# Two-layer graph network on one Trainium2 core: gate steps of the third pass one place earlier, and the mixing block's temporaries in the accumulator

## The chip, the cores and the metric

The kernel runs on one core of one Trainium2 chip. A time is that of one execution on the device, in microseconds (us), lower is better. A core has five engines with instruction streams of their own: TensorE (PE, matmuls; its weight loads are listed as PEld), VectorE (DVE), ScalarE (ACT), GpSimd (POOL) and SyncE (SP). [...] An engine takes its instructions strictly in the order in which they stand, so one that waits holds up all behind it.

## The reference

Two layers of a graph network over 6250 nodes with 256 features and 106250 edges, sorted by destination. Each layer adds to x a graph part, a mixing part and a feed-forward part. The change lies in the second layer:

```python
xn = _layernorm(x, axis=-1)
x = x + _L1_gnn_ref(xn, L1_gnn_W_self, L1_gnn_W_neigh, L1_gnn_b, src, dst) + _L1_mix_ref(xn[None], L1_mix_w_qkv, ...)[0]
x = x + _L1_ffn_ref(_layernorm(x, axis=-1)[None], L1_ffn_sW1, ...)[0]

# in _L1_mix_ref, over all nodes at once
attn = jax.nn.softmax(jnp.einsum('bhnd,bhne->bhde', k, v), axis=-1)
x = x + xf                                 # xf = attn applied to q
h = _layernorm(x, norm_g, norm_b)
h = jax.nn.gelu(h @ w_fc1 + b_fc1, approximate=False) @ w_fc2 + b_fc2

# in _L1_ffn_ref: one shared MLP and 4 experts, of which 2 count
gates = jax.nn.softmax(x @ gW + gb, axis=-1)
topv, topi = jax.lax.top_k(gates, TOPK)
topw = jax.nn.softmax(topv, axis=-1)
gated = jnp.sum(sel * topw[:, :, None, :], axis=-1)
return shared + gated
```

The graph part is a mean over each node's incoming edges of the rows of xn @ W_neigh, plus xn @ W_self + b.

## The kernel before

The nodes are 49 tiles of 128 rows (`T`), kept in the tile `XN`. The edges are 880 groups of 128, called visits (`VIS`). The kernel is a row of blocks. A block begins when all engines have ended the one before.

Three blocks are passes over the 880 visits, the third for the second layer. For each visit GpSimd fetches 128 source rows of 256 floats from a table in memory into one of 16 slots of the tile `rows` (line 1847), TensorE multiplies them with a 128x128 matrix of zeros and ones (line 1940), and VectorE adds the product to its place in `ACC`, the first 12544 columns of the large tile `AR` (line 2056). The profile shows each fp32 matmul as two. The results of two visits share a PSUM bank, two banks alternate, and VectorE adds a pair when its second visit is done. TensorE may begin a pair when the pair before the last one has been added (`s_av`, `x - 2`).

Beside the visits each pass does the dense work of the tiles. `turns` (line 732) sets the order, the same on every engine: turn `i` has places q = 0 to 17 and one place `QN` at the end; at each place first `side(i, q)` is issued, then one visit (18 or 19 to a turn, 18.3 on average). In turn `i` the third pass serves tile `i + 1` (`na`) for the mixing block's front and its norm, tile `i` (`b`) for its MLP, tile `i - 1` (`s`) for the norm ahead of the feed-forward part, and tile `i - 2` (`f`) for that part. An even or odd start of the turn's visits decides at which places the pairs end.

The chain of one tile `f` runs over all engines:

- TensorE q = 3: the gate's logits (L1978) into bank 7, and the first layer's product group 0 (`first_ffn`, L1955); q = 4: groups 1, 2; q = 5: group 3, then a wait until VectorE has read the logits (`lg`), since group 4 writes the same part of bank 7; then group 4; q = 6: group 5.
- VectorE q = 4: gate steps 0 and 1 (L2100, L2102; the second signals `lg`); q = 6: steps 2, 3; q = 7: steps 4, 5; q = 8, 9: steps 6 to 9; q = 10: `weights` (ends with L2135 and the signal `wg`). ScalarE takes the two exponentials at q = 5 and q = 8.
- TensorE q = 12: transposes the gate weights (L2013, waits for `wg`). VectorE q = 13: copies them out of PSUM (L2174, signals `wtc`). TensorE q = 14: spreads them (L2023, waits for `wtc`). VectorE q = 15: applies them (L2178).

Of another kind is the short block before the third pass (from line 1702): a serial chain of small matmuls and copies that makes the mixing block's 256x512 matrix from sums over all nodes. Its weights and temporaries lie in `rows`. GpSimd clears `ACC` there (line 1719). TensorE begins when all eight loads of the block have landed and GpSimd's three fills are done (lines 1731, 1732). The gathers of the third pass begin in the next block, since they write `rows`.

## Time and profile before

| | |
|---|---|
| median of 3 runs | 4081.71 us (4075.95 to 4083.36) |
| profiled execution | 4071.0 us |
| its span | 4069.3 us |
| mean granted TensorE clock | 0.895 |
| PE busy | 3277.6 us (81%) |
| DVE busy | 2367.5 us (58%) |
| ACT busy | 1846.6 us (45%) |
| POOL busy | 2698.7 us (66%) |

All rows come from the one profiled execution. Times are from the start of its span. Busy shares over the whole span are averages over stages with different limits. In this execution the short block begins at 2767.3 us and the third pass at about 2811 us, and the last instruction ends a few microseconds before 4069.3 us.

### The profile page before, as it was taken

The numbers are of one execution on the slowest core, as the hardware profiler recorded it, in microseconds if no ns is written. First come the engines' busy times: TensorE is split into PE (matmuls) and PEld (weight loads), VectorE is DVE, ScalarE is ACT, GpSimd is POOL, SyncE is SP. The second block draws the span as 40 slices with busy tenths as digits, with TensorE's granted clock in tenths as the row PEclk, the third lists the DMA queues.
The fourth block names the chain that finished last, engine by engine and source line by source line (L and its number), as shares of the span: only waits on it lengthen the run. The fifth ranks groups of instructions, "written<-read, shape, count | busy, mean of one in ns | idle before, by whom it ended". The sixth has DMA issues, their size and how long they took to land. (4 is left out here: it accounts for less than half of the span.)

```text
span 4069.3 us, 58095 instructions
## 1 busy us (share of the span) xinstructions
PE 3277.6 (81%) x15028; PEld 2486.5 (61%) x15028; DVE 2367.5 (58%) x8479; ACT 1846.6 (45%) x4614; POOL 2698.7 (66%) x2858
## 2 busy tenths in 40 slices
PE   7767666766666787888888888776999999999998
PEld 4544444444444465666667666664777777777777
DVE  6444444444444455666666665363777777777776
ACT  4344444444443444544445442132555555555554
POOL 4177777777776777777777773043776676666762
PEclk9677877787877788999999998886999999999999
DMA  4353333333333434666666666642333333333331
GB/s 123 95 159 111 112 110 111 110 112 110 110 112 97 118 120 141 192 194 203 200 193 197 194 193 223 201 136 75 109 104 101 101 102 102 101 101 101 103 101 48
DMA packets 268651, 532.12 MB, mean 131 GB/s; under 512 B 57942, under 2 KB 165653, under 8 KB 268199
## 3 DMA queue, kind: packets, MB, share of 16 engines
q0 software_dynamic: 139296, 386.65, 32.2%
q1 hardware_dynamic: 129030, 141.78, 11.0%
q8 instruction: 126, 2.06, 0.2%
q14 instruction: 199, 1.62, 0.1%
HBM read 463.88 MB, written 64.34 MB: 130 GB/s over the span
## 5 line engine op out<-in xcount | busy, mean ns | idle before, releaser
L1847 POOL DMA_INDIRECT rows<-table,src_idx x880 | 845.0, 960 | 388.2 <-issue 219.9
L786 POOL DMA_INDIRECT rows<-table,src_idx x880 | 835.3, 949 | 268.1 <-issue 265.4
L1061 POOL DMA_INDIRECT rows<-table,src_idx x880 | 835.2, 949 | 267.9 <-issue 253.5
L880 DVE TENSOR_TENSOR AR<-AR,ps 128x256 f32 x880 | 370.6, 421 | 592.3 <-PE ps L837 529.1
L1224 DVE TENSOR_TENSOR AR<-AR,ps 128x256 f32 x880 | 370.1, 421 | 329.1 <-PE ps L1135 244.4
L1940 PE MATMUL ps<-rows,AR 128*128 128x256 f32 x1760 | 538.6, 392 | 7.9 <-issue 3.6
L2056 DVE TENSOR_TENSOR AR<-AR,ps 128x256 f32 x880 | 369.2, 420 | 177.2 <-PE ps L1940 101.6
L837 PE MATMUL ps<-rows,work 128*128 128x256 f32 x880 | 315.0, 486 | 172.9 <-DMA rows<-table,src_idx 151.7
L1135 PE MATMUL ps<-rows,work 128*128 128x256 f32 x1168 | 362.6, 419 | 74.4 <-DMA rows<-table,src_idx 64.9
L837 PEld LDWEIGHTS ps<-rows,work 128*128 128x128 f32 x880 | 188.0, 238 | 272.2 <-issue 141.9
L1940 PEld LDWEIGHTS ps<-rows,AR 128*128 128x128 f32 x1760 | 285.8, 193 | 72.0 <-issue 50.3
L1135 PEld LDWEIGHTS ps<-rows,work 128*128 128x128 f32 x1168 | 221.5, 208 | 151.6 <-issue 105.0
L797 ACT ACTIVATE work<-iota,dst_rel 128x128 f32<-128x128 f32 x440 | 140.5, 390 | 231.7 <-PE ps L837 231.4
L837 PE MATMUL ps<-rows,mring 128*128 128x256 f32 x440 | 163.8, 501 | 100.5 <-DMA rows<-table,src_idx 92.5
L1135 PE MATMUL ps<-rows,mring 128*128 128x256 f32 x592 | 186.7, 420 | 72.0 <-DMA rows<-table,src_idx 66.0
L1176 PE MATMUL ps<-wreg,work 128*128 128x512 f32 x392 | 209.3, 662 | 30.1 <-DVE work L1328 15.2
L1111 ACT ACTIVATE AR<-AR 128x1024 f32<-128x1024 f32 x49 | 51.8, 1057 | 393.9 <-DVE AR L1341 393.9
L837 PE MATMUL ps<-rows,gates 128*128 128x256 f32 x440 | 163.6, 500 | 83.1 <-DMA rows<-table,src_idx 67.7
L1092 ACT ACTIVATE work<-iota,dst_rel 128x128 f32<-128x128 f32 x584 | 185.8, 391 | 84.1 <-PE ps L1135 84.1
L1955 PE MATMUL ps<-AR 128*128 128x128 f32 x1176 | 176.0, 282 | 22.5 <-DVEq L2104 21.6
L837 PEld LDWEIGHTS ps<-rows,mring 128*128 128x128 f32 x440 | 97.3, 245 | 153.7 <-issue 79.6
L1955 PEld LDWEIGHTS ps<-AR 128*128 128x128 f32 x1176 | 159.9, 191 | 37.2 <-DVEq L2104 29.0
(508 smaller groups left out, 6687.0 us busy)
## 6 DMA issues: line engine op xcount, KB each, us to landing
AR<-in_L_ffn_Wd SPq DMA_DIRECT2D x48, 1024.0 KB, 7.2
rows<-table,src_idx POOLq DMA_INDIRECT x2640, 2.8
AR<-h_sorted SPq DMA_DIRECT2D x52, 512.0 KB, 3.9
table<-AR SPq DMA_DIRECT2D x147, 128.0 KB, 2.2
AR<-in_x SPq DMA_DIRECT2D x4, 1536.0 KB
out_x<-XN SPq DMA_DIRECT2D x48, 128.0 KB
AR<-in_L_ffn_bd SPq DMA_DIRECT2D x40, 128.0 KB, 8.3
y_sorted<-AR SPq DMA_DIRECT2D x40, 128.0 KB
```

The costliest lines, as they stand in the source:

```text
L786: g.indirect_dma_start(out=rows[:, u * D:(u + 1) * D], out_offset=None, in_=table[0], in_offset=bass.IndirectOffsetOnAxis(ap=src_idx[:, x: ...
L837: ins = pe.matmul(pair(x), hot[Q % 4][:, x % 4 * P:(x % 4 + 1) * P], rows[:, x % RING * D:(x % RING + 1) * D], start=True, stop=True)
L880: v.tensor_tensor(acc, acc, pair(y), ALU.add).then_inc(s_av, 1)
L1061: g.indirect_dma_start(out=rows[:, u * D:(u + 1) * D], out_offset=None, in_=table[1], in_offset=bass.IndirectOffsetOnAxis(ap=src_idx[:, x: ...
L1092: ins = a.activation(hot[Q % 3][:, k * P:(k + 1) * P], iota[:, :], ACT.Abs, scale=-1.0, bias=dst_rel[:, 4 * Q + k:4 * Q + k + 1])
L1135: ins = pe.matmul(pair(x), hot[Q % 3][:, x % 4 * P:(x % 4 + 1) * P], rows[:, x % RING * D:(x % RING + 1) * D], start=True, stop=True)
L1176: ins = pe.matmul(ps[3 + h][:, :], f_xT[:, c * P:(c + 1) * P], ff1[:, c, h * 512:(h + 1) * 512], start=c == 0, stop=c == 1)
L1224: v.tensor_tensor(acc, acc, pair(y), ALU.add).then_inc(s_av, 1)
L1847: g.indirect_dma_start(out=rows[:, u * D:(u + 1) * D], out_offset=None, in_=table[2], in_offset=bass.IndirectOffsetOnAxis(ap=src_idx[:, x: ...
L1940: ins = pe.matmul(ps[x // 2 % 2][:, x % 2 * D:(x % 2 + 1) * D], hot[Q % 4][:, x % 4 * P:(x % 4 + 1) * P], rows[:, u * D:(u + 1) * D], star ...
L1955: ins = pe.matmul(f_l1(k), w, f_xT[:, c * P:(c + 1) * P], start=c == 0, stop=c == 1)
L2056: v.tensor_tensor(acc, acc, ps[x // 2 % 2][:, y % 2 * D:(y % 2 + 1) * D], ALU.add).then_inc(s_av, 1)
```

## The change

Five edits, all in the second layer's last two blocks.

1. TensorE: product group 4 and the wait for `lg` go from q = 5 to q = 6; the transpose of the gate weights goes from q = 12 to q = 11.
2. VectorE: gate steps 4, 5 go from q = 7 to q = 6, steps 6 to 9 from q = 8, 9 to q = 7, 8, `weights` from q = 10 to q = 9, and the copy of the gate weights from q = 13 to q = 12.
3. ScalarE: the second exponential goes from q = 8 to q = 7.
4. Short block: its large temporaries lie in the first 3856 columns of `ACC`, and the first 16 gathers of the third pass are issued there. GpSimd's order is: two small fills, 16 gathers, then zeros over the columns of `ACC` from 3856 on. TensorE waits for three of the eight loads (`s_wq`) and two fills.
5. Third pass: VectorE clears the first 3856 columns of `ACC` as its first instruction and waits for that.

```diff
+        s_gr = [sem(f"j_g{u}") for u in range(RING // 2)]
+        ATMP = 3856
+
+        def gather3(g, x):
+            u = x % RING
+            g.indirect_dma_start(out=rows[:, u * D:(u + 1) * D], out_offset=None, in_=table[2],
+                                 in_offset=bass.IndirectOffsetOnAxis(ap=src_idx[:, x:x + 1], axis=0)).then_inc(s_gr[u // 2], 16)
-        wqkv = rows[:, 0:1536].rearrange("p (c n) -> p c n", c=2)
+        wqkv = ACC[:, 0:1536].rearrange("p (c n) -> p c n", c=2)
...
             @block.gpsimd
             def _(g):
-                g.memset(ACC, 0.0).then_inc(s_z3, 1)
-                g.memset(rows[:, 3072:3328], 0.0).then_inc(s_z3, 1)
+                g.memset(ACC[:, 3072:3328], 0.0).then_inc(s_z3, 1)
                 g.memset(nval, float(N)).then_inc(s_z3, 1)
+                for x in range(RING):
+                    gather3(g, x)
+                g.memset(ACC[:, ATMP:T * D], 0.0).then_inc(s_z3, 1)
...
             @block.tensor
             def _(pe):
-                pe.wait_ge(s_w, 8 * 16)
-                pe.wait_ge(s_z3, 3)
+                pe.wait_ge(s_wq, 3 * 16)
+                pe.wait_ge(s_z3, 2)
...
@@ third pass, ScalarE @@
-                    if q == 8 and has(f):
                         a.wait_ge(*pr.after(f))
                         a.wait_ge(*wg.room(f))
                         a.activation(x4, p4, ACT.Exp, bias=n2).then_inc(e2.sem, 1)
@@ third pass, TensorE @@
                     if q == 5 and has(f):
                         first_ffn(f, (3,)).then_inc(l1a.sem, 1)
+                    if q == 6 and has(f):
                         pe.wait_ge(*lg.after(f))
-                        first_ffn(f, (4,))
-                    if q == 6 and has(f):
-                        first_ffn(f, (5,)).then_inc(l1.sem, 1)
+                        first_ffn(f, (4, 5)).then_inc(l1.sem, 1)
...
-                    if q == 12 and has(f):
                         pe.wait_ge(*wg.after(f))
                         pe.transpose(ps[7][0:NG + 1, D:D + P], f_w, ident[:, :]).then_inc(wt.sem, 1)
@@ third pass, VectorE @@
+                v.memset(ACC[:, 0:ATMP], 0.0).then_inc(s_az, 1)
+                v.wait_ge(s_az, 1)
...
                     if q == 6 and has(f):
-                        gate(f, 2)
-                        gate(f, 3)
-                    if q == 7 and has(f):
-                        gate(f, 4)
-                        gate(f, 5)
-                    if q in (8, 9) and has(f):
-                        gate(f, 2 * q - 10)
-                        gate(f, 2 * q - 9)
-                    if q == 10 and has(f):
+                        for k in range(2, 6):
+                            gate(f, k)
+                    if q in (7, 8) and has(f):
+                        gate(f, 2 * q - 8)
+                        gate(f, 2 * q - 7)
+                    if q == 9 and has(f):
                         weights(f)
...
-                    if q == 13 and has(f):
+                    if q == 12 and has(f):
                         v.wait_ge(*wt.after(f))
                         v.wait_ge(*l3.room(f))
                         v.tensor_copy(f_wT, ps[7][0:NG + 1, D:D + P]).then_inc(wtc.sem, 1)
```

In the listings of order below, a line number is that of its own program, so the same instruction has another one in the changed kernel. TensorE, places 3 to 7 of a turn in the middle of the pass, before (L1940 a visit, L1978 logits, L1955 the groups, two matmuls each, L1993 the mixing matrix):

```order
L1978 MATMUL ps<-AR 128x4 x2
L1955 MATMUL ps<-AR 128x128 x2
L1940 MATMUL ps<-rows,AR 128x256
L1955 MATMUL ps<-AR 128x128 x4
L1940 MATMUL ps<-rows,AR 128x256
L1955 MATMUL ps<-AR 128x128 x4
L1940 MATMUL ps<-rows,AR 128x256
L1955 MATMUL ps<-AR 128x128 x2
L1940 MATMUL ps<-rows,AR 128x256
L1993 MATMUL ps<-AR 128x512 x2
```

The same places now (L1949 a visit, L1987 logits, L1964 groups, L2001 mixing matrix):

```order
L1987 MATMUL ps<-AR 128x4 x2
L1964 MATMUL ps<-AR 128x128 x2
L1949 MATMUL ps<-rows,AR 128x256
L1964 MATMUL ps<-AR 128x128 x4
L1949 MATMUL ps<-rows,AR 128x256
L1964 MATMUL ps<-AR 128x128 x2
L1949 MATMUL ps<-rows,AR 128x256
L1964 MATMUL ps<-AR 128x128 x4
L1949 MATMUL ps<-rows,AR 128x256
L2001 MATMUL ps<-AR 128x512 x2
```

The wait for `lg` stood inside the third L1955 row, ahead of its second group; now it stands behind the third visit, ahead of the fourth L1964 row. TensorE, places 11 to 14, before (L2006, L2008 the second layer, L2013 the transpose of the gate weights, L2017 the mixing MLP's second product, L2023 the spreading):

```order
L2006 MATMUL ps<-AR 128x128 x2
L2008 MATMUL ps<-AR 128x128 x4
L1940 MATMUL ps<-rows,AR 128x256
L2013 MATMUL ps<-ident,AR 5x128
L1940 MATMUL ps<-rows,AR 128x256
L2017 MATMUL ps<-wreg,AR 128x256 x2
L1940 MATMUL ps<-rows,AR 128x256
L2017 MATMUL ps<-wreg,AR 128x256 x2
L2023 MATMUL ps<-AR 128x128 x2
```

And now (L2014, L2016, L2020, L2024, L2030 in that order):

```order
L2014 MATMUL ps<-AR 128x128 x2
L2016 MATMUL ps<-AR 128x128 x4
L2020 MATMUL ps<-ident,AR 5x128
L1949 MATMUL ps<-rows,AR 128x256 x2
L2024 MATMUL ps<-wreg,AR 128x256 x2
L1949 MATMUL ps<-rows,AR 128x256
L2024 MATMUL ps<-wreg,AR 128x256 x2
L2030 MATMUL ps<-AR 128x128 x2
```

The transpose has passed one visit; the spreading stands where it stood. VectorE, places 12 and 13 of a turn whose pairs end at odd places, before (L980, L975, L977 steps of two norms, L2174 the copy of the gate weights, L2056 the adding of a visit):

```order
L980 SCALAR_TENSOR_TENSOR gsml<-gsml 128x1
L975 TENSOR_SCALAR gsml<-gsml 128x1
L977 SCALAR_TENSOR_TENSOR gsml<-gsml 128x1 x2
L980 SCALAR_TENSOR_TENSOR gsml<-gsml 128x1
L977 SCALAR_TENSOR_TENSOR gsml<-gsml 128x1
L2174 COPY AR<-ps 5x128
L2056 ISA
L2056 TENSOR_TENSOR AR<-AR,ps 128x256
```

And now (L2180 the copy, L2065 the adding):

```order
L980 SCALAR_TENSOR_TENSOR gsml<-gsml 128x1
L975 TENSOR_SCALAR gsml<-gsml 128x1
L977 SCALAR_TENSOR_TENSOR gsml<-gsml 128x1
L2180 COPY AR<-ps 5x128
L977 SCALAR_TENSOR_TENSOR gsml<-gsml 128x1
L980 SCALAR_TENSOR_TENSOR gsml<-gsml 128x1
L977 SCALAR_TENSOR_TENSOR gsml<-gsml 128x1
L2065 ISA
L2065 TENSOR_TENSOR AR<-AR,ps 128x256
```

The copy has passed three norm steps. In a turn whose pairs end at even places it passes the two adds of a pair as well.

## Rows read from the trace of the kernel before

**Rows 1.** A stretch: from:to, us, busy us of each engine, granted clock, DMA.
```profile
3300.00:3500.00 200.00, 187.86 (x1071) 153.93 (x1069) 147.74 (x579) 107.20 (x280) 140.41 (x146) 1.00 0.35 101
```
**Rows 2.** Waits, 2900 to 4069 us: waiter, releaser, us in total, times, longest.
```profile
POOL rows L1847 <- PE ps L1940: 133.7, 153, 2.9
DVE AR L2056 <- PE ps L1940: 93.2, 132, 2.5
PE ps L2023 <- DVE AR L2174: 36.3, 44, 1.5
PE ps L1955 <- DVEq L2104: 21.6, 35, 1.2
PE ps L2013 <- DVEq L2137: 5.6, 12, 0.5
```
**Rows 3.** PE in order of time: start, us, what [idle before, releaser].
```profile
3576.29 0.60 PE L1940 MATMUL ps<-rows,AR 128*128 128x256 f32 x2
...
3580.50 0.71 PE L1955 MATMUL ps<-AR 128*128 128x128 f32 x4 [0.52 <-DVEq L2104]
3581.05 0.60 PE L1940 MATMUL ps<-rows,AR 128*128 128x256 f32 x2
3581.48 0.61 PE L1955 MATMUL ps<-AR 128*128 128x128 f32 x4
...
3594.40 0.71 PE L2023 MATMUL ps<-AR 5*128 5x128 f32 x4 [1.18 <-DVE AR L2174]
...
3971.70 0.71 PE L2023 MATMUL ps<-AR 5*128 5x128 f32 x4 [1.32 <-DVE AR L2174]
```
**Rows 4.** DVE in order of time, the same turn.
```profile
3575.10 0.96 DVE L2056 TENSOR_TENSOR AR<-AR,ps 128x256 f32 x2
...
3581.78 0.97 DVE L2056 TENSOR_TENSOR AR<-AR,ps 128x256 f32 x2 [1.02 <-PE ps L1940]
...
3593.49 0.35 DVE L977 SCALAR_TENSOR_TENSOR gsml<-gsml 128x1 f32<-128x1 f32 x2
...
3594.08 0.27 DVE L2174 COPY AR<-ps 5x128 f32<-5x128 f32 x1
```
**Rows 5.** DVE, a turn whose pairs end at even places.
```profile
3389.88 0.97 DVE L2056 TENSOR_TENSOR AR<-AR,ps 128x256 f32 x2
...
3391.23 0.27 DVE L2174 COPY AR<-ps 5x128 f32<-5x128 f32 x1
```
**Rows 6.** Short block in order of time, all engines.
```profile
2767.32 10.55 POOL L1719 MEMSET AR<- 128x12544 f32 x1 [33.15 <-POOLq L1538]
...
2778.21 0.18 PEld L1734 LDWEIGHTS ps<-ident,rows 128*128 128x128 f32 x1 [14.06 <-DMA wreg<-in_L_mix_b_fc]
2778.24 0.45 PE L1734 MATMUL ps<-ident,rows 128*128 128x128 f32 x1 [13.69 <-POOL rows L1721]
...
2789.35 0.69 DVE L1778 COPY rows<-ps 128x512 f32<-128x512 f32 x1 [9.27 <-PE ps L1745]
...
2809.30 0.69 DVE L1809 TENSOR_TENSOR AR<-AR 128x512 f32<-128x512 f32 x1
```
**Rows 7.** DMA from 2765 to 2812 us, 40 slices of 1.175 us.
```profile
GB/s 144 79 32 230 392 236 369 327 365 79 0 0 0 0 0 0 0 0 0 0 0 0 0 0 0 0 0 0 0 0 0 0 0 0 0 0 0 0 0 0
```
**Rows 8.** Start of the third pass in order of time, all engines.
```profile
2812.44 0.94 POOL L1847 DMA_INDIRECT rows<-table,src_idx  x1 [0.30 <-issue]
2813.69 0.94 POOL L1847 DMA_INDIRECT rows<-table,src_idx  x1 [0.30 <-issue]
...
2818.17 0.69 DVE L2160 TENSOR_TENSOR AR<-ps,AR 128x512 f32<-128x512 f32 x1 [6.02 <-PE ps L1993]
...
2861.09 0.67 PE L1940 MATMUL ps<-rows,AR 128*128 128x256 f32 x2 [1.27 <-DMA rows<-table,src_idx]
```
**Rows 9.** Two stretches at low clock, columns as in rows 1.
```profile
2884.70:2888.10 3.40, 3.40 (x9) 2.25 (x8) 2.81 (x9) 0.00 (x0) 2.79 (x3) 0.51 0.39 112
3973.50:3980.30 6.80, 6.80 (x16) 4.58 (x15) 3.43 (x12) 0.00 (x0) 3.26 (x4) 0.50 0.16 45
```

More of the change, by code:

```diff
@@ L1680, in _ @@
                         v.sem_inc(s_nf, 1)
-        wqkv = rows[:, 0:1536].rearrange("p (c n) -> p c n", c=2)
-        gram = rows[:, 1536:2048].rearrange("p (c n) -> p c n", c=2)
-        t1 = rows[:, 2048:2560].rearrange("p (c n) -> p c n", c=2)
-        wq1T = rows[:, 2560:3072].rearrange("p (c n) -> p c n", c=2)
-        abd = rows[:, 3072:3328].rearrange("p (c n) -> p c n", c=2)
-        abT = rows[:, 3328:3584].rearrange("p (c n) -> p c n", c=2)
-        bqc = rows[:, 3584:3586]
-        bqm = rows[:, 3600:3728]
-        csum, nmx = rows[:, 3586:3588], rows[:, 3588:3590]
-        rsm = rows[:, 3590:3592]
-        nval = rows[0:1, 3592:3593]
-        att = rows[:, 3728:3856].rearrange("p (c n) -> p c n", c=2)
+        s_gr = [sem(f"j_g{u}") for u in range(RING // 2)]
[5 more added lines that the diff above has]
+        wqkv = ACC[:, 0:1536].rearrange("p (c n) -> p c n", c=2)
+        gram = ACC[:, 1536:2048].rearrange("p (c n) -> p c n", c=2)
+        t1 = ACC[:, 2048:2560].rearrange("p (c n) -> p c n", c=2)
+        wq1T = ACC[:, 2560:3072].rearrange("p (c n) -> p c n", c=2)
+        abd = ACC[:, 3072:3328].rearrange("p (c n) -> p c n", c=2)
+        abT = ACC[:, 3328:3584].rearrange("p (c n) -> p c n", c=2)
+        bqc = ACC[:, 3584:3586]
+        bqm = ACC[:, 3600:3728]
+        csum, nmx = ACC[:, 3586:3588], ACC[:, 3588:3590]
+        rsm = ACC[:, 3590:3592]
+        nval = ACC[0:1, 3592:3593]
+        att = ACC[:, 3728:3856].rearrange("p (c n) -> p c n", c=2)
         bqkv = work[0:1, 0:768]
@@ L1777, in _ @@
                 v.wait_ge(s_p, 5)
-                link(v.tensor_copy(rows[:, 2048:2560], ps[1][:, :]))
+                link(v.tensor_copy(ACC[:, 2048:2560], ps[1][:, :]))
                 link(v.tensor_copy(t2row, ps[2][0:1, 0:D]))
@@ L1786, in _ @@
                 v.wait_ge(s_p, 8)
-                link(v.tensor_copy(rows[:, 2560:3072], ps[4][:, :]))
+                link(v.tensor_copy(ACC[:, 2560:3072], ps[4][:, :]))
                 v.wait_ge(s_a, 2)
@@ L1797, in _ @@
                 v.wait_ge(s_p, 10)
-                link(v.tensor_copy(rows[:, 3328:3584], ps[5][:, 0:D]))
+                link(v.tensor_copy(ACC[:, 3328:3584], ps[5][:, 0:D]))
                 v.wait_ge(s_p, 14)
@@ L1809, in _ @@
                 link(v.tensor_tensor(gws[:, :, D:2 * D], gws[:, :, D:2 * D], gws[:, :, 0:D], ALU.add))
-        s_gr = [sem(f"j_g{u}") for u in range(RING // 2)]
+        s_az = sem("j_acc_zero")
         s_mv, s_av, s_abs, s_hota, s_hotv = (sem("j_" + n) for n in "visit added abs hot_a hot_v".split())
@@ L1842, in _ @@
             def _(g):
-                for x in range(VIS):
-                    u = x % RING
-                    if x >= RING and x % 2 == 0:
+                for x in range(RING, VIS):
+                    if x % 2 == 0:
                         g.wait_ge(s_mv, (x + 2 - RING) // 2)
-                    g.indirect_dma_start(out=rows[:, u * D:(u + 1) * D], out_offset=None, in_=table[2],
-                                         in_offset=bass.IndirectOffsetOnAxis(ap=src_idx[:, x:x + 1], axis=0)).then_inc(s_gr[u // 2], 16)
+                    gather3(g, x)
             @block.scalar
```

14 lines of the change are left out of this document (8 added, 6 removed).

## The prediction

> **What bounds the kernel now.** I read first the busy times by stretch, to see which engine is near its limit in the stage that the change touches; then the waits of that stage, summed; then one turn in order of time on TensorE and on VectorE; last the short block and its DMA traffic.
>
> [...] GpSimd issues a gather every 1.25 us if it waits for nothing [rows 8]: 22.9 us a turn. It isn't the bound, and it waits for TensorE 133.7 us in all [rows 2]. TensorE's own waits are the three last lines of rows 2: 36.3 us for the copy of the gate weights, 21.6 us for gate step 1 (`lg`), 5.6 us for `weights`. [...] So TensorE bounds the pass, held up by VectorE at two places of each turn where VectorE happens to be late, while at other places VectorE waits for it. [...]
>
> **The wait for the copy (L2174).** In the turn shown TensorE stands 1.18 us before L2023, and goes on 0.32 us after the copy starts [rows 3, 4]. The copy now stands ahead of three norm steps: 3593.62 instead of 3594.08 (the second of the two L977 that start at 3593.49), so 0.46 us sooner. In a turn whose pairs end at even places it also passes the two adds: 3389.88 instead of 3391.23, 1.35 us sooner [rows 5]. Half the turns are of each kind. The same view for all 46 turns with visits gives waits of 0.88 us on average in the 24 turns of the second kind, of which about 20.5 us in all go, and 0.74 us in the 22 of the first kind, of which 0.45 us go each, 10 us. Together 30 of some 38 us. The copy can't be held up by its own input: the transpose ahead of it moves one place too.
>
> **The wait for `lg`.** It moves behind one visit, 0.43 us of TensorE work (3581.05 to 3581.48) [rows 3]. 35 waits make 21.6 us [rows 2]; each loses 0.43 us or all it has: 14 us go, some 7 stay. Group 4 isn't needed sooner, since `l1` was signalled behind group 5 before as well. Behind the wait that is now at q = 6 stand groups 4, 5 and the next visit, as many as before less one.
>
> **The wait for `weights`** (L2013). On VectorE `weights` passes the place q = 9 with its norm steps and often a pair's adds (0.97 us, rows 4), on TensorE the transpose passes one visit (0.43 us). So it gains more than it loses: 5 of the 5.6 us go. The moved gate steps cost no new time. Until q = 9 VectorE does about 0.8 us more of its work than before, and has it less afterwards. Before the adds at q = 5 it stands idle for 1.02 us in the turn shown [rows 4], and the visit there now runs ahead of TensorE's wait instead of behind it, so those adds can begin sooner. If that idle time were not there, the 0.8 us would push the adds back; they would still be ahead of the visit that needs them, two pairs later. ScalarE takes its exponential one place sooner, at 54% busy: nothing.
>
> First order: 30 + 14 + 5 = 49 us.
>
> **What is late next.** The end of a turn on VectorE. In the turn shown the last pair's adds end at 3575.10 + 0.96 = 3576.06, and the third visit of the next turn, which needs them, starts at 3576.29 [rows 3, 4]: 0.23 us of room. TensorE comes some 0.85 us sooner at q = 14 and VectorE not by all of it. I take that 0.5 us come back as a new wait in each of the 22 turns of this kind, 11 us. Less than nothing can't come back. At the other end VectorE keeps its idle places and all that the copy's move brings TensorE from q = 14 on comes back, 0.8 us in each of 46 turns, 37 us. So the pass gives 38 us, bounds 12 and 50.
>
> **The short block.** TensorE starts at 2778.24, when GpSimd's fill of 10.55 us and the two small ones are done; the loads are also just down, its weight load names one of them [rows 6]. Now it needs two small fills and three loads, 0.79 MB. By its slices, from the first load at about 2767.7 [rows 7], 0.27, 0.46 and 0.28 MB move until 2769.7, 2770.9 and 2772.05, so these three are down at about 2771.1 and, with the 1.3 us that lie between the end of traffic (2776.9) and the start at 2778.2, seen at 2772.4: 5.8 us sooner. The gathers are beside them now, 128 KB every 1.25 us or 105 GB/s against some 300: about 1.3 us later. I take 4.5 us; the bounds are 0 (the loads no sooner than all eight were) and 5.8. The chain behind, to the end of L1809 at 2809.99 [rows 6], is the same instructions on other columns. GpSimd needs 0.4 us of fills, 16 x 1.25 = 20 us of gathers and 10.55 x 8688/12544 = 7.3 us of zeros, so it ends near 2795, 10 us ahead of the chain. VectorE's zeros over 3856 columns are not in the trace; by the copies of 512 columns in 0.69 us [rows 6] some 4 to 5 us, between bounds of 2 and 8 us. They lie at the start of the pass, where VectorE stands idle 6.02 us before L2160 [rows 8], so I take 0; at 8 us they would cost 2.
>
> [...] If gathers and weights shared evenly for the whole load, the three loads would take up to twice their 3.4 us and the block's gain would be 2 instead of 4.5 us. No row of the kernel before has both in flight there.
>
> **The first turns.** With 16 rows fetched early the wait of 1.27 us for a gather at 2861.09 [rows 8] goes: 1.3 us.
>
> **The clock.** [...] TensorE is busy through both stretches, so they cost up to half of 10.2 us. I take 2 us, bounds 0 and 5. [...]
>
> **Sum.** 38 + 4.5 + 1.3 + 2 = 46 us off the profiled execution's 4071.0, so 4025 for such an execution. Its own time is 10.7 us under the median of the three runs, which spread over 7.4 us; the forecast goes by the median: 4081.7 - 46 = 4036 us. About 0.2%, 8 us, is what a measurement of this kernel can tell from no change.
>
> **Rivals.**
> 1. *VectorE becomes the bound.* [...] Against it: its idle places at q = 5 and q = 7 are filled by the change itself. Then the pass gives 12 to 25 us and the rest 2 to 6: a gain of about 22, 4060 us. Chance 0.18.
> 2. *The waits come back elsewhere.* TensorE gets to L2023 sooner and stands as long for the next thing that VectorE, as late as before, delivers: the spread weights' use or the norm's rows. Only the short block and the first turns stay, a gain of 6: 4076 us. For it: VectorE's chain from q = 8 to q = 13 runs with hardly a pause. Against it: the copy itself passes work in every turn, by the listing of order. Chance 0.07.
> 3. *Slower: the turn's end on VectorE.* Its place is the adds of a turn's last pair and the third visit. If the denser gate work leaves VectorE later there by more than the 0.23 us of room plus the 1.07 us a turn (49/46) that the moves give, TensorE stands longer than before. At 0.4 us beyond that point the 46 turns cost 18 us, less 6 of the block: 4094 us. For it: the narrow room. Against it: no instruction is added to a turn. Chance 0.05.
>
> The forecast has 0.70, with its own range 4020 to 4052. The range reaches from 4016 (50 + 5.8 + 1.3 + 5 off, and 4 us for the spread of the medians) to 4068, which takes in most of rival 1. Faster by over 0.2%: 0.70 + 0.18 and 0.01 of rival 2, 0.89. Within 0.2%: 0.07. Slower: 0.04.
>
> **What would show it.** In the new waits the line of the spreading matmuls (L2030) has under 12 us, the one of the product groups on gate step 1 under 10, the transpose near 0. TensorE's first matmul of the short block comes 5 to 8 us after GpSimd's first fill instead of 10.9, and 16 gathers stand in that block. A turn in the middle takes 24.3 us, 1.32 us a visit, with TensorE busy 96 to 97%. A new group of waits of a visit's matmul on the adds shows the part given back, about 11 us. The prediction is wrong if these waits are above 25 us, if the waits for the copy stay, if the short block is no shorter, or if the pass loses its full clock.

## The result, and the profile after

| | before | changed |
|---|---|---|
| median | 4078.83 us (4069.96 to 4083.36, 4 runs) | 4006.7 us (4004.6 to 4010.86, 4 runs) |
| ratio, 95% interval | | 0.9827 (0.9807 to 0.9847) |
| profiled execution | 4071.0 us | 4010.9 us |
| span, mean granted clock | 4069.3 us, 0.895 | 4009.1 us, 0.895 |
| GpSimd's first fill in the short block to the end | 1302.0 us | 1239.2 us |

The kernel is faster by 72 us of the medians in this comparison, where 46 were forecast; the time lies below the forecast's own range (4020 to 4052 us) and below the wider one (from 4016 us). A second comparison (below) gave 66 us. The last row of the table is the steadiest measure: up to the first fill of the short block all kernels here are the same, and that fill came anywhere between 2753.2 and 2769.9 us in eleven profiled executions, while the stretch behind it repeats within 0.5 us (before 1302.0 and 1301.5, changed 1239.2 and 1239.1). By it the change is worth 62.4 to 62.8 us, at the lower end of the first comparison's interval (62 to 79 us) and inside the second's (56 to 70 us).

The middle of the third pass, the stretch of [rows 1]:

```profile
3300.00:3500.00 200.00, 196.02 (x1134) 162.26 (x1135) 153.88 (x607) 114.04 (x299) 147.31 (x154) 1.00 0.38 107
```

TensorE is busy 98%, was 94%, and there are 154 gathers instead of 146: 1.30 us a visit, was 1.37. The mean of 46 turns went from 25.32 to 24.05 us (24.3 forecast). The waits from 2900 us on, as in [rows 2]; first the groups of waits, then the group of the visits' matmuls, whose last figures are the idle time ahead of it, of before (L1940) and after (L1949):

```profile
POOL rows L1688 <- PE ps L1949: 68.7, 115, 1.2
DVE AR L2065 <- PE ps L1949: 21.9, 55, 1.1
PE ps L1964 <- DVEq L2113: 5.2, 16, 0.7
PE ps L2030 <- DVE AR L2180: 3.3, 8, 0.5
```
```profile
L1940 PE MATMUL ps<-rows,AR 128*128 128x256 f32 x1636 | 499.1, 389 | 1.5 <-issue 1.3
```
```profile
L1949 PE MATMUL ps<-rows,AR 128*128 128x256 f32 x1628 | 491.2, 388 | 8.0 <-issue 7.1 <-DVE AR L2065 0.2
```

The copy's wait fell from 36.3 to 3.3 us, that for gate step 1 from 21.6 to 5.2, the transpose's is gone. 6.5 us came back ahead of the visits. VectorE waits for the visits' matmuls 21.9 us instead of 93.2. It is still TensorE that bounds the pass, so rivals 1 and 3 of the prediction did not come.

The short block, all engines, against [rows 6]; the last row answers to the memset that had no row before:

```profile
2769.91 0.31 POOL L1728 MEMSET AR<- 128x256 f32 x1 [33.14 <-POOLq L1538]
...
2775.51 0.47 PE L1745 MATMUL ps<-ident,AR 128*128 128x128 f32 x1 [8.35 <-DMA AR<-in_L_mix_b_qkv]
...
2790.38 7.36 POOL L1732 MEMSET AR<- 128x8688 f32 x1
...
2795.66 2.11 DVE L1796 TENSOR_SCALAR AR<-AR 128x2 f32<-128x2 f32 x1
...
2808.53 0.69 DVE L1821 TENSOR_TENSOR AR<-AR 128x512 f32<-128x512 f32 x1
...
2811.53 3.27 DVE L2046 MEMSET AR<- 128x3856 f32 x1 [2.31 <-issue]
```

TensorE starts 5.6 us after the first fill, was 10.9. But L1796, an operation on 2 columns, takes 2.11 us, and it ends 0.03 us after GpSimd's fill (2797.74). So the chain ends 39.3 us after the first fill instead of 42.7: 3.4 us sooner, not 5.3.

### The profile page after: what moved, and what is told of

Read it like the earlier page. It is cut to its first block and busy times, and to the rows that moved or that the text cites. A ratio compares the mean times of both kernels' runs of the same rounds, so it can differ in the third digit from the quotient of the medians.

```text
span 4009.1 us, 58097 instructions
## 1 busy us (share of the span) xinstructions
PE 3268.3 (82%) x15028; PEld 2483.5 (62%) x15028; DVE 2371.8 (59%) x8480; ACT 1843.5 (46%) x4614; POOL 2701.9 (67%) x2858
## 5 line engine op out<-in xcount | busy, mean ns | idle before, releaser
L1949 PE MATMUL ps<-rows,AR 128*128 128x256 f32 x1760 | 532.4, 391 | 12.6 <-issue 10.4
L2065 DVE TENSOR_TENSOR AR<-AR,ps 128x256 f32 x880 | 368.8, 419 | 110.3 <-PE ps L1949 25.9
L1949 PEld LDWEIGHTS ps<-rows,AR 128*128 128x128 f32 x1760 | 287.2, 192 | 82.9 <-issue 58.3
L837 PE MATMUL ps<-rows,mring 128*128 128x256 f32 x440 | 160.6, 493 | 93.2 <-DMA rows<-table,src_idx 82.1
L1158 PE MATMUL ps<-AR 128*128 128x256 f32 x640 | 172.3, 397 | 9.8 <-DMA AR<-in_L_ffn_bd 9.8
L837 PEld LDWEIGHTS ps<-rows,gates 128*128 128x128 f32 x440 | 96.3, 241 | 131.7 <-issue 71.0
```

Source lines behind the costliest of these rows:

```text
L837: ins = pe.matmul(pair(x), hot[Q % 4][:, x % 4 * P:(x % 4 + 1) * P], rows[:, x % RING * D:(x % RING + 1) * D], start=True, stop=True)
L1158: ins = pe.matmul(ps[6][:, 0:D], XHT[:, k * P:(k + 1) * P], XW[b % 2][:, k * D:(k + 1) * D], start=k == 0, stop=k == HC - 1)
L1949: ins = pe.matmul(ps[x // 2 % 2][:, x % 2 * D:(x % 2 + 1) * D], hot[Q % 4][:, x % 4 * P:(x % 4 + 1) * P], rows[:, u * D:(u + 1) * D], star ...
L2065: v.tensor_tensor(acc, acc, ps[x // 2 % 2][:, y % 2 * D:(y % 2 + 1) * D], ALU.add).then_inc(s_av, 1)
```

## The experiments

All ratios are to the kernel before, measured in the same session. The sessions fell under two conditions: under the first the kernel before takes 4072 to 4074 us as in the result, under the second 4677 to 4686. The record gives a chip number with every session of experiments, and number 1 stands with both conditions, so it is not shown that the two are two chips.

For most of the runs under the first condition I took TensorE's matmuls in order of time from the q = 0 transposes of tile 2 to those of tile 48, 46 turns, called turns 2 to 48 below by that tile. Each gap of over 0.02 us is put down to the line behind it (us; "low clock" is the time at a granted clock of 0.50 within these turns; "rest" is the length less the idle time and half the low clock):

| kernel | copy | gate step 1 | transpose | visits, first 7.5 us of a turn | visits, later | all idle | low clock | rest | length | first fill to end |
|---|---|---|---|---|---|---|---|---|---|---|
| before | 36.9 | 21.6 | 6.0 | 6.2 | 1.4 | 77.1 | 13.7 | 1080.7 | 1164.7 | 1302.0 |
| before_again | 36.8 | 21.8 | 6.0 | 6.2 | 1.0 | 77.3 | 6.8 | 1081.8 | 1162.5 | 1301.5 |
| lg_again | 37.1 | 7.1 | 6.1 | 6.4 | 1.4 | 63.2 | 23.9 | 1078.4 | 1153.5 | 1290.4 |
| dvecopy12 | 1.8 | 22.5 | 17.4 | 6.8 | 0.9 | 54.5 | 0 | 1079.4 | 1133.9 | 1272.2 |
| copy_again | 3.7 | 22.9 | 0 | 6.6 | 6.4 | 44.5 | 3.4 | 1079.5 | 1125.7 | 1262.5 |
| moves_again | 3.4 | 7.1 | 0 | 6.6 | 5.4 | 27.4 | 3.4 | 1078.0 | 1107.2 | 1243.6 |
| after_again | 3.3 | 6.3 | 0 | 6.2 | 5.8 | 26.9 | 3.4 | 1077.6 | 1106.2 | 1239.1 |
| weights_behind | 0.3 | 6.3 | 0 | 7.5 | 1.7 | 21.0 | 0 | 1074.3 | 1095.2 | 1229.6 |

**after_again and before_again.** The two kernels unchanged.

> The changed kernel once more, on a chip where its parts were or can be timed. Theory A (the parts add: the moves' waits, the short block and nothing else): its gain over the kernel before is that of the moves plus that of the block, so 21 + 16 = 37 to 45 us on a chip like the one of the single edits (ratio 0.990 to 0.992), and 60 to 72 us on one like that of the first result. Theory B (part of the gain comes only when all edits stand together, because TensorE then waits nowhere long enough for the clock to dip): more than the sum by 10 us or more. In the profile both expect under 30 us of idle time of TensorE in turns 2 to 48 on a chip like the first, against 77 before; theory B also expects no stretch at 0.5 in the third pass, where the kernel before has one or more.

> The kernel before once more, for its profile on this chip beside those of the other kernels. Nothing changed: ratio 1.000 within 0.3%. If the dips of the granted clock in the third pass are chance, they lie elsewhere or are not there; if they follow the waits for the copy, there are one or more again, each behind a wait of over 1.2 us on L2023.

4007.09 us, ratio 0.9845 (0.9828 to 0.9862), 63 us; the kernel before gave 0.9996 (0.9984 to 1.0008). The gain is 62.4 us by profile; moves_again beside it has 57.9. So 4.5 us are left for the short block and for whatever comes only when all edits stand together, and theory B's 10 us are ruled out. The waits of before repeat to 0.2 us.

**moves_again.** Edits 1 to 3 alone, the third pass's order:

```diff
-                    if q == 13 and has(f):
+                    if q == 12 and has(f):
                         v.wait_ge(*wt.after(f))
...
```

> Gate steps, copy of the gate weights and product group moved; temporaries, zeros and gathers as in the kernel before. By the prediction's working the moves bring 38 to 40 us. By the account of the two first traces (turns 2 to 48 shorter by 58 us, of which 50 are idle time of TensorE that is gone and 8 a shorter busy time) they bring 58 us, a ratio of 0.9858, on a chip like that of the first result; the rest of the change is then worth 4 to 6 us. On a chip where the before kernel takes 4677 us they brought 21 to 26 us.

4015.58 us, ratio 0.9862 (0.9845 to 0.9879), 56 us. The moves bring 56 to 58 us, the short block and the early gathers the other 4.5 by profile. The short block's edits were not run alone under the first condition.

**lg_again.** One wait and one product group:

```diff
                     if q == 5 and has(f):
                         first_ffn(f, (3,)).then_inc(l1a.sem, 1)
+                    if q == 6 and has(f):
                         pe.wait_ge(*lg.after(f))
-                        first_ffn(f, (4,))
-                    if q == 6 and has(f):
-                        first_ffn(f, (5,)).then_inc(l1.sem, 1)
+                        first_ffn(f, (4, 5)).then_inc(l1.sem, 1)
```

> The kernel before with the wait for gate step 1 and product group 4 moved behind one visit, nothing else. The prediction gave this edit 14 us (35 waits, 0.43 us each or all they have). By the two accounts of TensorE (waits on that line 21.7 us before, 6.3 after, all edits together) 15 us. Rival (VectorE then delivers the later steps no sooner, and the 0.4 us a turn come back at the copy and the transpose): those two lines wait 37 + 6 us before and over 50 here, and the time is 0 to 6 us shorter. On a chip where the kernel before takes 4073 us: ratio 0.9963 if the edit keeps its 15 us, 0.999 by the rival.

Ratio 0.9963 (0.9949 to 0.9976), 15 us. The wait fell from 21.8 to 7.1 us and nothing came back at the copy or the transpose. Its profiled execution gained only 11 us; it has 17.1 us more low clock than before_again. It shows the clock: four stretches at half clock in the pass (columns as in rows 1), and on TensorE's spreading matmul the wait ahead of each:

```profile
2886.20:2889.60 3.40, 3.40 (x9) 2.31 (x8) 2.81 (x9) 0.00 (x0) 2.77 (x3) 0.50 0.39 116
3063.70:3070.50 6.80, 6.80 (x16) 4.59 (x15) 3.63 (x11) 1.32 (x4) 3.34 (x4) 0.50 0.19 58
3241.20:3248.00 6.80, 6.80 (x16) 4.57 (x15) 3.73 (x12) 1.56 (x4) 3.23 (x4) 0.50 0.17 46
3964.80:3968.20 3.40, 3.40 (x9) 2.68 (x10) 1.90 (x8) 0.00 (x0) 1.84 (x2) 0.50 0.25 72
```
```profile
2884.73 0.71 PE L2022 MATMUL ps<-AR 5*128 5x128 f32 x4 [1.58 <-DVE AR L2173]
3061.65 0.71 PE L2022 MATMUL ps<-AR 5*128 5x128 f32 x4 [1.53 <-DVE AR L2173]
3239.39 0.71 PE L2022 MATMUL ps<-AR 5*128 5x128 f32 x4 [1.53 <-DVE AR L2173]
3964.02 0.71 PE L2022 MATMUL ps<-AR 5*128 5x128 f32 x4 [1.45 <-DVE AR L2173]
```

Each stretch begins 0.8 to 2.1 us after a wait of 1.45 to 1.58 us for the copy. In the three executions with that wait in its old place (before, before_again, lg_again) there are seven such stretches from turn 3 on, all behind waits for the copy of 1.24 us or more. Five waits for the copy of over 1.5 us have none behind them, nor have two waits ahead of a visit of 2.4 and 2.2 us early in turn 3. In the eight executions under this condition with the copy moved there is none between turn 3 and the pass's last 6 us. So in these runs a fall to 0.50 follows some of the waits of 1.24 to 1.58 us and not others; what decides between them is not shown.

**dvecopy12.** Only the transpose and the copy go one place forward; gate steps and `weights` stay:

```diff
-                    if q == 12 and has(f):
                         pe.wait_ge(*wg.after(f))
                         pe.transpose(ps[7][0:NG + 1, D:D + P], f_w, ident[:, :]).then_inc(wt.sem, 1)
...
-                    if q == 13 and has(f):
+                    if q == 12 and has(f):
```

> The kernel before with only the transpose (q = 12 to 11 on TensorE) and the copy (q = 13 to 12 on VectorE) moved; gate steps, weights and exponential stay. Tells whether the copy's place alone took away the waits, or the gate steps had to come sooner. Theory A (place alone): the copy's waits fall from 36.8 to under 10 us; the transpose now comes 0.43 us sooner upon weights that come no sooner, so its waits rise from 6 by at most 46 x 0.43 = 20 to at most 26; net 15 to 25 us off, ratio 0.994 to 0.996. Theory B (the chain of gate steps is what the copy waited for): the waits move to the transpose in full, 6 to 35 or more, and the time is 0 to 8 us shorter.

Ratio 0.9923 (0.9911 to 0.9936), 31 us. TensorE's waits on the transpose and the copy in the third pass, of this kernel:

```profile
PE ps L2012 <- DVEq L2136: 17.4, 28, 0.9
...
PE ps L2022 <- DVE AR L2173: 1.3, 4, 0.3
```

Theory A holds: the place alone took 35 us of waits off the copy, of which 11.4 us came back at the transpose. The idle time fell by 22.8 us, within the range given; the time fell by more (28.6 us in these turns), since 3.4 us went with the low clock and 2.4 us of the rest went too.

**copy_again.** The same with gate steps, `weights` and exponential moved, group 4 where it was:

```diff
                     if q == 6 and has(f):
-                        gate(f, 2)
-                        gate(f, 3)
...
+                        for k in range(2, 6):
+                            gate(f, k)
...
-                    if q == 10 and has(f):
+                    if q == 9 and has(f):
                         weights(f)
```

> The kernel before with the gate steps, weights, transpose, copy and exponential moved, and group 4 where it was. The prediction: 30 + 5 us for the waits, 11 given back at the turn's end, 1 to 2 for the clock: 25 us. By the accounts (waits for copy and transpose 43 before, 3.3 after; visits' waits 7.4 before, 12.0 after; dip of the clock 1206 us into the stage gone): 40 - 4.6 + 3.4 + overhang of the removed waits 2 = 41 us, ratio 0.9900. If the part given back depends on the other edit too, visits wait over 12 us here and gate step 1 (L1954 here) over 21.8.

Ratio 0.9908 (0.9893 to 0.9924), 37 us; 39.0 by profile. Against dvecopy12 it takes 17.4 us off the transpose and puts 5.5 on the later visits. So the part given back belongs to the edit of the gate steps and `weights`, and comes late in the turn. The visits wait 13.0 us in all and gate step 1 22.9 us. Both are about 1 us over the marks (12 and 21.8) at which part of it would depend on the other edit too, so a share of about 1 us is not excluded. The gains of this run and of lg_again add up to 52 us, against 56 of both edits together.

**zeros_mid and late_gathers.** Two places for GpSimd's work in the short block. The first puts the fill between the eighth and the ninth gather, the second holds the gathers back:

```diff
-                for x in range(RING):
+                for x in range(RING // 2):
                     gather3(g, x)
                 g.memset(ACC[:, ATMP:T * D], 0.0).then_inc(s_z3, 1)
+                for x in range(RING // 2, RING):
+                    gather3(g, x)
```
```diff
                 g.memset(nval, float(N)).then_inc(s_z3, 1)
+                g.wait_ge(s_wq, 3 * 16)
                 for x in range(RING):
```

> The changed kernel with GpSimd's fill of the accumulator (128x8688, 7.36 us) between the eighth and the ninth early gather instead of behind the sixteenth. Theory: VectorE's tensor_scalar L1796 (SBUF to SBUF, 128x2) took 2.11 us in the changed kernel because it can't go on while GpSimd fills; it ended 0.03 us after the fill. Between the eighth and ninth gather (about 2780.6 to 2788 us) VectorE has only copies out of PSUM, which the fill did not slow. Then L1796 takes 0.17 us and the short block ends 1.9 us sooner: 1.9 us less in all, too little for the times to tell from no change (ratio to the changed kernel 0.9995), but read off the profile. Rival (the 2.11 us is a wait of another kind, for its own input or ScalarE's table load): L1796 takes 2 us again. If copies out of PSUM are held up as well, L1789 at about 2786.6 takes up to 2 us instead of 0.69.

> The changed kernel with GpSimd's sixteen early gathers held back until the three loads that the short block needs are down. In the changed kernel TensorE started 5.60 us after GpSimd's first fill. The prediction took 1.3 us off for gathers beside the loads; if so TensorE starts at 4.3 us here. By even sharing between the queues it would start up to 3.4 us sooner, near 2.2 to 3. If packets of the gathers cost the loads nothing: 5.6 again. The gathers then end about 5 us later, GpSimd's fill at 33 instead of 28 us into the block, on top of more of VectorE's steps (L1804, L1808, SBUF to SBUF): if the fill holds those up as it did L1796, one of them takes 2 to 7 us and the block is longer; it ends at 39.3 us in the changed kernel.

zeros_mid: 4012.42 us, ratio 0.9855 (0.9838 to 0.9872). In order of time, fill and step:

```profile
2778.02 7.36 POOL L1732 MEMSET AR<- 128x8688 f32 x1
...
2784.48 0.69 DVE L1791 COPY AR<-ps 128x512 f32<-128x512 f32 x1 [9.27 <-PE ps L1758]
...
2793.50 0.17 DVE L1798 TENSOR_SCALAR AR<-AR 128x2 f32<-128x2 f32 x1
```

late_gathers: 4015.36 us, ratio 0.9862 (0.9847 to 0.9877):

```profile
2764.19 0.31 POOL L1728 MEMSET AR<- 128x256 f32 x1 [33.16 <-POOLq L1538]
...
2769.84 0.47 PE L1746 MATMUL ps<-ident,AR 128*128 128x128 f32 x1 [8.41 <-DMA AR<-in_L_mix_b_qkv]
2770.06 0.97 POOL L1688 DMA_INDIRECT rows<-table,src_idx  x1 [5.53 <-DMA AR<-in_L_mix_b_qkv]
...
2789.79 7.36 POOL L1733 MEMSET AR<- 128x8688 f32 x1
2789.99 7.18 DVE L1797 TENSOR_SCALAR AR<-AR 128x2 f32<-128x2 f32 x1
```

One thing is shown. The step takes 0.17 us without a fill beside it, 2.11 when the fill is nearly over and 7.18 when it has just begun, and ends within 0.03 us of the fill's end both times; the copy out of PSUM (L1791 above), with the fill beside it, takes the same 0.69 us as without one. In late_gathers the step stands in the chain with its whole 7.18 us: the chain ends 44.4 us after the first fill, 5.1 us later than in the changed kernel, and from the first fill to the end it takes 1247.0 us, 7.9 us more.

The loads are another matter. With no gather issued beside them TensorE starts 5.65 us after the first fill; in the changed kernel, with four issued, 5.60 us; the prediction's 1.3 us for them was 0. But the gathers' rows (q0) had hardly begun to move. These are the packets and MB of each queue in the first 4 us of the changed kernel's short block (2769.9 to 2773.9 us):

```profile
q1 hardware_dynamic: 512, 0.77, 63.5%
q0 software_dynamic: 16, 0.07, 7.7%
```

So the two kinds of traffic were not in flight together for long, and whether they would share evenly if they were is not shown by these runs.

zeros_mid's chain ends 37.7 us after the first fill, 1.6 us sooner, yet the stage is 1.3 us longer (1240.5 us): the table's turns 2 to 48 take 1108.4 us there, and two stretches of 6.8 us at half clock lie in the first turns where the changed kernel has one of 3.4. late_gathers has the same two. I could not show that these are all of the loss.

**weights_behind.** The last run, on what makes the later visits wait. VectorE at q = 9 in the kernel before, in the changed kernel, and in this one, in order of time:

```profile
3384.52 0.17 DVE L2125 TENSOR_REDUCE AR<-AR 128x4 f32<-128x16 f32 x1
3385.07 0.43 DVE L2165 TENSOR_TENSOR XN<-XN,AR 128x256 f32 x1 [0.38 <-issue]
```
```profile
3406.33 0.35 DVE L2144 TENSOR_SCALAR AR<-AR 128x4 f32<-128x4 f32 x1
3407.35 0.43 DVE L2171 TENSOR_TENSOR XN<-XN,AR 128x256 f32 x1 [0.67 <-DVE AR L2144]
...
3408.32 0.97 DVE L2065 TENSOR_TENSOR AR<-AR,ps 128x256 f32 x2
```
```profile
3422.12 0.21 DVE L977 SCALAR_TENSOR_TENSOR gsml<-gsml 128x1 f32<-128x1 f32 x1
3422.36 0.42 DVE L2169 TENSOR_TENSOR XN<-XN,AR 128x256 f32 x1
```

```diff
-                    if q == 9 and has(f):
-                        weights(f)
...
                         v.tensor_tensor(x, x, W2[:, D:2 * D], ALU.add).then_inc(s_xa, 1)
+                    if q == 9 and has(f):
+                        weights(f)
```

> The changed kernel with `weights` behind instead of ahead of the mixing block's residual add, both at q = 9 on VectorE. Theory: the register load ahead of the add can't overlap the last step of `weights` when that stands directly in front of it, so VectorE stands 31.0 us in 46 turns at the add; with other work in front it stands 17.7 us (as in the kernel before). Then the 13 us of VectorE's time come back, visits wait 12.0 - 4.6 = 7.4 us over turns 2 to 48 on a chip like the first, and the stage takes 1234 to 1236 us instead of 1239. The transpose at q = 11 gets its weights some 0.9 us later and waits up to 6 us in all, which could eat it. Rival (the visits behind wait because of the amount of work ahead of their adds, not of this gap): the gap closes and visits still wait 12 us. On the chip where the kernel before takes 4677 us only the gap (31.0 or 17.7 us) can be read.

3998.46 us, ratio 0.9819 (0.9801 to 0.9838), under the first condition. The idle time ahead of the residual add over the third pass, of the changed kernel run again and of this one:

```profile
DVE XN L2171 <- DVE AR L2144: 31.0, 46, 0.7
```
```profile
L2169 DVE TENSOR_TENSOR XN<-XN,AR 128x256 f32 x47 | 20.1, 427 | 3.2 <-issue 1.7
```

31.0 us (17.7 in the kernel before) became 3.2, the later visits' waits fell from 5.8 to 1.7 us, and the copy's from 3.3 to 0.3. From the first fill to the end it takes 1229.6 us, 9.5 less than the changed kernel, of which 1.7 are low clock. The gap closed and the visits stopped waiting, so the rival falls; the gap closed further than I expected. That it is the register load is read from the kernel and not tested by itself: `weights` ends with a wait for its own last step, the load (0.31 us, L178) stands behind that wait, and the add behind the load. No run takes away the load or the wait alone. It is the fastest version here. By the times alone it is not told apart from the changed kernel (the intervals 0.9801 to 0.9838 and 0.9828 to 0.9862 overlap, and the two ran in different comparisons); the profile tells them apart.

**Under the second condition.** Nine runs: moves (as moves_again), block_only (edits 4 and 5 alone), lg_only, copy_only (as the two above), and three variants, two of them twice over. The gate steps lumped at q = 7 instead of q = 6 (gates_q7, gates_q7b), the fill between the twelfth and the thirteenth gather (zeros_late, zeros_lateb), and both:

```diff
-                        for k in range(2, 6):
+                        gate(f, 2)
+                        gate(f, 3)
+                    if q == 7 and has(f):
+                        for k in range(4, 8):
                             gate(f, k)
-                    if q in (7, 8) and has(f):
-                        gate(f, 2 * q - 8)
-                        gate(f, 2 * q - 7)
+                    if q == 8 and has(f):
+                        gate(f, 8)
+                        gate(f, 9)
```
```diff
-                for x in range(RING):
+                for x in range(RING - 4):
                     gather3(g, x)
                 g.memset(ACC[:, ATMP:T * D], 0.0).then_inc(s_z3, 1)
+                for x in range(RING - 4, RING):
+                    gather3(g, x)
```

> The moves of edits 1 to 3 alone; the short block and the start of the pass stay as before. Theory A (the moves carry nearly all, by themselves): 56 to 62 us faster than before, in the pass TensorE's idle time falls from 77 to about 28 us and its busy time by about 8 us. Theory B (the rows that the changed kernel fetches early let TensorE run ahead, and the moves need that): 35 to 50 us faster, and waits of L1931 or its like for gathers appear. The rest to the changed kernel is the block: 3 to 5 us by A, over 12 by B.

> Edits 4 and 5 alone (temporaries in the accumulator, 16 gathers early, zeros shared between two engines), with the pass's order as before. Theory A: 3 to 6 us faster, TensorE starts about 5.5 us after the block's first instruction instead of 10.9, turn length 25.2 us as before. Theory B (early rows help the pass): over 12 us faster, with turns shorter than 25 us. No gain at all if the VectorE zeros or the contention eat it.

> Edit 1's first half alone: group 4 and the wait for gate step 1 from q = 5 to q = 6, all else as before. Theory A: the waits there fall from 21.6 to 6 us, and each wait that goes takes the refilling of TensorE with it, so 15 to 20 us faster. Theory C (the visit that now runs ahead of the wait lets VectorE add its pair sooner, which carries on to the copy, the transpose and the turn's end): 25 us or more, with the waits for the copy down too. Theory D (VectorE takes it back later): under 10 us.

> Edits 2 and 3 with the transpose (gate steps, weights, transpose, copy, exponential one place sooner), without the move of group 4. Theory A (sum of parts): 38 to 44 us faster, waits for the copy near 4 us, those for gate step 1 still about 21. Theory D' (the turn's end on VectorE gives back what the forecast said, 11 us, unless the adds at q = 5 come sooner by the other move): 25 to 33 us, with new waits of the visits on the adds of 10 us or more, and waits for gate step 1 above 25.

> The changed kernel with the four gate steps that stand together one place later: steps 2 and 3 at q = 6, 4 to 7 at q = 7, 8 and 9 at q = 8, weights at q = 9 as in the changed kernel. If the waits of visits (12 us over turns 2 to 48, 5 more than without the edit) come from the lump of four steps at q = 6, they move or fall to 7 to 9 us, and the third pass is 3 to 5 us shorter than in the changed kernel (from the first fill to the end 1239 us there). If they come from `weights` one place sooner (with adds and norm steps behind it), they stay at 12. If the steps now end later than `weights` can use them, the transpose waits again, over 3 us.

> The changed kernel with GpSimd's fill of 7.36 us between the twelfth and the thirteenth early gather, 15.4 to 22.8 us into the block; VectorE's steps out of SBUF begin at 25. Expected by all theories: L1796 takes 0.17 us and TensorE's first visit comes 1.6 to 2 us sooner in the block than in the changed kernel. If the 1.9 us gained were lost to the phase of the clock in the other such kernel, the same two low stretches of 6.8 us in the first turns show here or not, and the time from first fill to end is 1240 with them and 1237 without; if the gathers behind the fill cost it, 1240 us without such stretches.

> Gate steps 4 to 7 at q = 7 and the fill between the twelfth and the thirteenth gather. If both points bring what they may: 1233 us from first fill to end, 6 us or 0.15% under the changed kernel; if each brings nothing: 1239 to 1240.

| kernel | ratio, 95% interval |
|---|---|
| moves | 0.9944 (0.9924 to 0.9964) |
| block_only | 0.9962 (0.9944 to 0.9980) |
| lg_only | 0.9982 (0.9969 to 0.9995) |
| copy_only | 0.9969 (0.9954 to 0.9984) |
| gates_q7, gates_q7b | 0.9928 (0.9912 to 0.9945), 0.9939 (0.9919 to 0.9959) |
| zeros_late, zeros_lateb | 0.9929 (0.9912 to 0.9946), 0.9917 (0.9891 to 0.9943) |
| both | 0.9923 (0.9902 to 0.9944) |

The moves are worth under half there (26 us by the ratio, 21 by the medians). A stretch of the pass and TensorE's first waits in it, of moves (second condition) and then of moves_again:

```profile
3300.00:3900.00 600.00, 532.50 (x2881) 423.52 (x2881) 397.06 (x1536) 286.78 (x750) 378.75 (x394) 0.97 0.32 91
```
```profile
PE ps L1939 <- issue: 20.9, 27, 3.3
PE ps L1954 <- issue: 16.4, 9, 3.7
PE ps L1939 <- DVE AR L2053: 9.9, 10, 1.7
```
```profile
3300.00:3900.00 600.00, 586.76 (x3386) 484.78 (x3384) 463.67 (x1814) 340.35 (x890) 438.31 (x457) 1.00 0.37 107
```
```profile
PE ps L1977 <- ACT AR L1879: 3.5, 4, 0.9
PE ps L1939 <- issue: 3.1, 10, 0.5
```

TensorE is busy 89% there instead of 98, and stands up to 3.7 us at a time for something that the profile doesn't name. In turns 2 to 48 the clock is at 0.50 for 72 to 89 us, under the first condition for 0 to 24. Between lg_only and moves the copy's and the transpose's waits of turns 2 to 48 fall from 93 to 12 us as they should, and 51 us come back ahead of the visits (16.8 to 67.7) and 17 ahead of the logits (12.3 to 29.3). So most of the gain comes back elsewhere, as in the second rival of the prediction; why it does is not shown.

block_only gained 18 us where 3 to 6 were expected. Its chain in the short block is 3.4 us shorter, as under the first condition. But from the end of that chain to turn 2 it takes 33.7 us, against 44.7 to 45.2 us in the three kernels without early gathers (30 to 32 us with or without them under the first condition). So the rows fetched early are worth some 11 us there and next to nothing under the first condition.

The three variants can't be told apart: the fill's place did give L1798 its 0.17 us (1.93 in block_only), but from first fill to end they take 1422 and 1424 us (zeros_late, zeros_lateb), 1426 and 1428 (gates_q7, gates_q7b) and 1430 (both), where two executions of one kernel differ by 2 us, and the changed kernel itself was not run under this condition. What makes it slower stays open.

## Why the prediction was wrong

The direction, the engine that bounds the pass and the places were right, the size was not: even the upper bound of 50 us for the pass was passed (33.5 + 15.5 + 6.0 - 4.8 + 4.2 = 54.4, the clock not counted). By its steps, against before_again and after_again:

| term | forecast | measured | from |
|---|---|---|---|
| wait for the copy | 30 | 33.5 | 36.8 - 3.3 |
| wait for gate step 1 | 14 | 15.5 | 21.8 - 6.3 |
| wait of the transpose | 5 | 6.0 | 6.0 - 0 |
| given back | -11 | -4.8 | (6.2 + 5.8) - (6.2 + 1.0) |
| clock | 2 | 1.7 (5.1 by the first pair) | half of 6.8 - 3.4 (of 13.7 - 3.4) |
| not in the sum | 0 | 4.2 | 1081.8 - 1077.6 |
| outside turns 2 to 48: short block, first turns | 5.8 | 6.1 | 62.4 - (1162.5 - 1106.2) |
| all | 46 | 62.4 | 1301.5 - 1239.1 |

- **The step that failed most** is "I take that 0.5 us come back as a new wait in each of the 22 turns of this kind, 11 us", at the turn's end on VectorE. Next to nothing came back there. In the first 7.5 us of a turn, where the third visit stands, visits wait 6.2 us before and 6.2 after. Of these 4.7 and 3.2 us lie in the first two of the 46 turns, so in the 44 others they went from 1.5 to 3.1 us, and those of the third visit itself from 0.4 to 1.2. The 0.23 us of room was no measure of VectorE's lateness. As I read it, VectorE, which waited for TensorE 2 us a turn, was held back by the same removed waits and came sooner with TensorE. The wait that was forecast is seen 4 times in these 44 turns (once before), as here in the changed kernel (VectorE's adds, then the third visit):

```profile
3370.46 0.97 DVE L2065 TENSOR_TENSOR AR<-AR,ps 128x256 f32 x2
```
```profile
3371.52 0.67 PE L1949 MATMUL ps<-rows,AR 128*128 128x256 f32 x2 [0.53 <-issue]
```

- **What did come back** is 4.8 us net, and 6.4 us without the first two turns. 4.9 us of it stand ahead of the visits at q = 12 and 13 and have a cause that the prediction had not seen: `weights`, moved to q = 9, stands directly ahead of a register load and an add, and VectorE idles 0.67 us there instead of 0.385. "The moved gate steps cost no new time" is the sentence that was wrong; weights_behind shows it.
- **The waits removed** were 3.5, 1.5 and 1 us more than forecast. For the copy the 0.45 us a turn forecast for the turns whose pairs end at odd places was too little: of 36.8 us only 3.3 are left in all. dvecopy12 has 35 of them gone with that edit alone, 11.4 of them to the transpose; the earlier gate steps and `weights` are what kept these from coming back there (copy_again has no wait left on the transpose).
- **Not in the sum at all** was that a wait costs more than its row. 42 waits of over 0.02 us fewer in turns 2 to 48 (122 to 80) left TensorE's time between them shorter by 4.2 us, 0.1 us each. In [rows 3] a visit is listed with 0.60 us but the next matmul starts 0.43 us after it: the 0.17 us of overlap is lost at a wait, and the row's idle time begins only behind it. I infer this from the rows. The other runs point the same way, not evenly: weights_behind has 60 waits and a rest of 1074.3 us, dvecopy12 97 and 1079.4, lg_again 105 and 1078.4. No run takes it apart.
- **The clock** was of the right size. The 2 us were the author's estimate between 0 and half of the 10.2 us of the two stretches of [rows 9]. Both stand behind a wait for the copy, of 1.53 us at 2883.32 and of 1.32 us at 3971.70; only that at 3973.5 came back in the second profile (3959.1, 1205.9 us after the first fill instead of 1206.2), behind a wait of 1.24 us.
- **The short block** was 3.4 us shorter in the first pair and 3.7 in the second, not 4.5: the start came 5.3 us sooner, since the 1.3 us taken off for contention did not come, and L1796 lost 2 us to the fill. The first turns gave 0.1 us in the first pair and 1.3 in the second. That the sum of the two, 5.8 us forecast and 6.1 measured, came out is luck: 1.1 us of the 6.1 lie behind turn 48, where nothing was forecast. VectorE's memset took 3.27 us (4 to 5 estimated) and was hidden: L2166 behind it still waited 1.88 us for TensorE.
- **The base.** The forecast went from 4081.7, the kernel before measured 4078.8 and 4073.5 later. The 62 us of the profiles agree with the 66 and 72 of the medians within the intervals, with the first just so.

## What to carry to other kernels

Where one engine bounds a stage and another waits for it, an edit that removes waits of the first can bring the second forward as well: don't price a new wait at every narrow gap between them (11 us were priced here, and the visits' waits in the first 7.5 us of a turn stayed at 6.2), but look for idle time that the moved instructions make by their new neighbours. Look at what stands directly behind a moved step on its own engine, here a register load and an add, and try other work between them: the idle time ahead of the add went from 31.0 to 3.2 us over the pass. When a fill goes to GpSimd, look in the trace at VectorE's operations beside it: here one of 0.17 us took 7.18 us beside a fill of 7.36 us.

## What the runs showed of the hardware that was not expected

- A 128x2 tensor_scalar on VectorE, 0.17 us without a fill beside it, took 2.11 and 7.18 us beside a fill of 7.36 us on GpSimd and ended with it within 0.03 us; a reduce (L1795 of the changed kernel) and a 128x512 copy out of PSUM (L1791 of zeros_mid) ran beside the fill at their usual 0.29 and 0.69 us.
- Gathers issued from 0.7 us after the first fill on, one every 1.25 us, had moved only 0.07 MB 4 us after it, and did not delay the 0.79 MB of loads beside them (5.60 against 5.65 us).
- The granted clock fell to 0.50 within 2.1 us of a wait of 1.24 to 1.58 us in a stage where TensorE is busy 94%, behind some such waits and not behind others; in the eight executions under the first condition with the copy moved it did not fall between turn 3 and the pass's last 6 us.
- The same kernel takes 4074 us in one session and 4677 in another, both under chip number 1 in the record. In the second TensorE has waits of up to 3.7 us that the profile gives no releaser for, and the same edits are worth 26 us instead of 56.
